# Depthwise convolution of the first batch: three tiles on TensorE in sixteen 32x32 array tiles, in place of one with 128x128 diagonals

## The chip, the cores and the metric

The kernel runs on one core of one Trainium2 chip. The metric is device time in microseconds (us), the lower the better. The measurement of this kernel can tell a change of about one per cent.

## What is computed

Two blocks in a row on x of shape (4, 256, 32, 32), all in float32:

```
# block 1, linear attention over heads of 8 channels
qkv = concat(wq, wk, wv) x                    # 768 channels
dw  = depthwise 5x5 convolution of qkv, SAME  # 25 taps per channel, weights per channel
pw  = 1x1 convolution of dw in groups of 8
f   = concat(qkv, pw) by heads: relu(query), relu(key), value with a column of ones
out = (value key^T) query, divided by its last row + 1e-15
y   = batch norm(proj out) + x
# block 2, attention over the 1024 pixels
out = o(h(y) softmax(f(norm y)^T g(norm y))) + y
```

## The kernel before

The four batch entries ("batches" 0 to 3) go through the core one after the other. The 768 channels of qkv are six tiles of 128 partitions: 0 and 1 hold the queries, 2 and 3 the keys, 4 and 5 the values. The images stand in `raw` with a border of zeros, so that a tap of the convolution is a shifted view (`tap_view`), and the sums go to `conv`.

Each engine has its order written out by hand; they meet at semaphores. `body(b)` is the stretch of one batch: pointwise convolution of keys and values (`pwkv`, L663), qkv of the next batch (`raw_kv`, L471 to L475), scores (L548), pointwise queries (`pwq`, L678 and L682), projection (L708), statistics and folding, then the attention of block 2: eight times energy (L605), softmax, transposes (L620) and values (L629). Ahead of `body(0)` stands a first stage for batch 0 alone: weights, qkv, and its convolution.

The convolution of batch b+1 runs beside `body(b)`, spread over three engines. VectorE multiplies and adds a tap in one instruction (`conv_taps`, L1143), for tiles 2, 3, 0 and the last eight taps of tile 1. For tiles 4 and 5 and seven taps of the shared tile 1, ScalarE makes a product (`conv_products`, L895) in one of five buffers, and GpSimd adds it (`conv_adds`, L1354); ScalarE waits for the addition that empties the buffer. Ten further taps of tile 1 ("late") go through ScalarE and GpSimd into a tile of their own inside `body(b)` (`late_products`, `late_adds`), and `pwq` adds that tile with a matrix product of its own (L682). Numbers in tables such as `FIRST_TAPS` say how many taps or products go between two other steps. The last `CARRY[b]` places of VectorE's list for batch b are done inside `body(b)`; the first 50 of the list are tiles 2 and 3.

Batch 0 has no body to hide its convolution, and divides it otherwise: tile 5 goes to TensorE. VectorE makes 25 diagonal matrices from the weights (L1314), and `diagonal_conv(h, first, last)` (L538) multiplies one half of the image, h, by one diagonal for each tap, all into one bank of PSUM; ScalarE copies it to `conv` (L924). The order on TensorE is

```
raw_q; diagonal_conv(0); scores; diagonal_conv(1, 0, 6); denominators; score_transposes;
diagonal_conv(1, 6, 12); fused_weights; spread 0; diagonal_conv(1, 12, 18); spread 1;
diagonal_conv(1, 18, 25); body(0)
```

Tile 1 of batch 0 has twelve taps on GpSimd in place of seven, and `body(0)` begins when VectorE has done tiles 2 and 3 and GpSimd all its 35 additions.

PSUM banks 0 to 3 are a ring (`a_slot`): each use has a running number, a bank is given out again when `a_free` has counted the use four numbers earlier, and `a_free` counts in order. `A_FIRST` is the number at the end of the first stage.

Of the kernel before, what the change touches and what calls it, by code (L numbers as in the profile page):

```python
# [6 lines left out]
ALU = mybir.AluOpType  # L7
# [5 lines left out]
P = 128  # L13
B = 4
C = 256
SIDE = 32
# [37 lines left out]
SHARED_TAPS, FIRST_SHARED_TAPS = 7, 12  # L54
# [8 lines left out]
PE_TILE = 5  # L63
PE_TAPS = [(PE_TILE, i) for i in range(NTAPS)]

SHARED_AT = 32

CARRY = (17, 16, 15, 2)
# [14 lines left out]
FIRST_POOL_SEQ = pool_order([tap for tap in ALL_TAPS if tap not in PE_TAPS], FIRST_SHARED_TAPS)  # L83
DVE_SEQ = [(t, i) for t in DVE_TILES for i in range(NTAPS) if (t, i) not in POOL_SEQ + LATE_SEQ]
DVE_TAPS, PRODUCTS = len(DVE_SEQ), len(POOL_SEQ)
KV_TAPS = sum(t not in Q_TILES for t, _ in DVE_SEQ)
# [4 lines left out]
POOL_ADDS = len(ADD_SEQ)  # L91
# [38 lines left out]
FIRST_TAPS = (42, 51, 57, 62)  # L130
FIRST_SPLIT = 29
# [5 lines left out]
FIRST_PRODUCTS_CONV = (16, 0)  # L137
FIRST_PRODUCTS_M = (3, 9, 15)
# [5 lines left out]
A_CONV = 2  # L144
CONV_BREAKS = (6, 12, 18)
# [12 lines left out]
def conv_seq_kernel(nc, x, wqkv, dw, pw, proj, bn, fgw, hw, ow, l1b, masks, out):  # L158
    with ExitStack() as ctx:
# [31 lines left out]
        mask_sb = sb("mask_sb", [P, 2 * P + HPT + CK * P])  # L191
# [18 lines left out]
        head_rows = mask_sb[:, 2 * P + HPT:].rearrange("p (h m) -> p h m", h=CK)  # L210
# [84 lines left out]
        def lay_out_mixed(b, at):  # L295
# [6 lines left out]
        a_end = lay_out(A_AT, [("raw_kv", A_RAWKV), ("kvt", A_KVT), ("raw_q", A_RAWQ), ("conv_0", A_CONV),  # L302
                               ("st_raw", 1), ("mb_raw", 1), ("conv_1", A_CONV)], 0, 0)
# [28 lines left out]
        def dve_count(b, n):  # L332
            return DVE_TAPS * b + n


        def product_count(b, n):
            return len(FIRST_POOL_SEQ) + (PRODUCTS + LATE) * b - PRODUCTS + n

        def add_count(b, n):
            return len(FIRST_ADD_SEQ) + (POOL_ADDS + LATE - 1) * b - POOL_ADDS + n  # L340

        def add_index(b, m):
            return add_count(b, m) if b else m
# [4 lines left out]
        def late_product_count(b, n):  # L348
            return product_count(b, PRODUCTS) + n

        def late_add_count(b, n):
            return add_count(b, POOL_ADDS) + n

# [26 lines left out]
        def conv_slot(h):  # L380

            return A_AT[f"conv_{h}", 0] + (A_CONV - 1 if h == 0 else 0)
# [20 lines left out]

        def diagonal(t, i):

            n = PE_TAPS.index((t, i))
            if n < 2 * NB:
                return ht[:, n // 2, n % 2 * P:(n % 2 + 1) * P]
            n -= 2 * NB
            return x1[:, n // NB, n % NB * P:(n % NB + 1) * P]  # L410
# [45 lines left out]
        def _(pe):  # L456
# [66 lines left out]
            def diagonal_conv(h, first, last):  # L523

                bank = a_bank(conv_slot(h))
                for i in range(first, last):
                    dst, view = square(bank), tap_view(PE_TILE, i)
                    y0, y1 = h * SIDE // 2, (h + 1) * SIDE // 2
                    if i > 0:

                        dy, dx = shift(i)
                        y0, y1 = max(y0, -dy), min(y1, SIDE - dy)
                        x0, x_end = max(0, -dx), SIDE - max(0, dx)
                        dst = dst[:, y0 - h * SIDE // 2:y1 - h * SIDE // 2, x0:x_end]
                        view = view[:, y0:y1, x0:x_end]
                    else:
                        view = view[:, y0:y1, :]
                    mm = pe.matmul(dst, diagonal(PE_TILE, i), view, start=(i == 0), stop=(i == NTAPS - 1))  # L538
                if last == NTAPS:
                    mm.then_inc(a_full, A_CONV)  # L540
# [113 lines left out]
            def body(b):  # L654
                with_next = b + 1 < B
                pe.wait_ge(conv_dve, dve_count(b, KV_TAPS))
# [14 lines left out]
                for i in range(A_PWQ):  # L671
# [7 lines left out]
                    if t == SHARED_TILE:  # L679
                        if h == 0:  # L680
                            pe.wait_ge(conv_pool, late_add_count(b, LATE - 1))
# [767 lines left out]
```

## Time and profile before

| | |
|---|---|
| time, median of 3 runs (lowest, highest) | 700.99 us (698.55, 703.51) |
| span of the profiled execution | 700.8 us |
| TensorE busy | 636.0 us (91%) |
| VectorE busy | 563.5 us (80%) |
| ScalarE busy | 470.7 us (67%) |
| GpSimd busy | 541.0 us (77%) |
| mean granted TensorE clock | 0.978 |

The profiled execution's own time is its span, 700.8 us; it lies 0.2 us under the median of the runs, so sums made on the span can be read as times. Busy shares are means over a first stage (to about 107 us), three bodies with the next batch's convolution beside them, and a last body without one, in which VectorE and ScalarE fall to two or three tenths and GpSimd stops. A float32 matrix product stands in the trace as two records, one for each pass; "PE" is the multiplication, "PEld" the load of its stationary operand.

### The profile page before, as it was taken

To read this page: it belongs to the slowest core of one execution; us is meant where nothing else is said; L and a number is where in the kernel's file an instruction comes from. 1 tells how busy PE (TensorE), PEld (TensorE's weight loads), DVE (VectorE), ACT (ScalarE), POOL (GpSimd) and SP (SyncE) were. 2 spreads that over 40 slices of the span, in tenths; PEclk is the share of its full clock that TensorE was granted. 3 is DMA by queue.
4 is the path that set the end of the run, shared out by engine and by line. 5 is a ranking of instruction groups with operands and counts; after the bars stand their busy time and mean duration, and the time that the engine had idled before them with its cause. 6 is when DMAs were issued, how large, how long until landed. Compare 5 with 4: busy or idle time off the path is not lost.

```text
span 700.8 us, 8645 instructions
## 1 busy us (share of the span) xinstructions
PE 636.0 (91%) x3176; PEld 475.3 (68%) x3176; DVE 563.5 (80%) x661; ACT 470.7 (67%) x745; POOL 541.0 (77%) x253
## 2 busy tenths in 40 slices
PE   4979978999989999999989999999898977997998
PEld 3854537665868787656778877648677773485887
DVE  5899899788989999989999998989999993442321
ACT  4787608897777769888676977987886662232231
POOL 4899996999999899999999999999999891000000
PEclk9979999999999999999999999999999998899999
DMA  8000001001010000001100000000100000000000
GB/s 296 2 0 1 0 0 61 1 1 34 27 61 15 16 31 1 0 1 60 61 1 16 16 31 1 1 0 1 61 15 16 9 22 1 0 1 0 16 16 30
DMA packets 6537, 16.23 MB, mean 23 GB/s; under 512 B 864, under 2 KB 992, under 8 KB 5984
## 3 DMA queue, kind: packets, MB, share of 16 engines
q1 hardware_dynamic: 6496, 15.69, 6.3%
q8 instruction: 25, 0.41, 0.2%
q14 instruction: 16, 0.13, 0.1%
HBM read 11.50 MB, written 4.19 MB: 22 GB/s over the span
## 4 chain that ended last, share of the span: by engine, by line
PE 36%; issue 20%; DVE 16%; ACT 15%; POOL 12%; DMA 1%; POOLq 0%; SPq 0%; DVEq 0%; ACTq 0%
DVE ps L1143 9%; PE ps L629 7%; PE ps L605 7%; ACT prod L895 7%; POOL conv L1354 7%; POOL rows L1354 4%; PE ps L538 4%; PE ps L708 3%; DVE small L1280 2%; PE ps L471 2%; PE ps L620 2%; ACT raw L864 1%; PE ps L756 1%; PE ps L475 1%; PE ps L472 1%
## 5 line engine op out<-in xcount | busy, mean ns | idle before, releaser
L1354 POOL TENSOR_TENSOR conv<-conv,prod 128x930 f32<-128x930 f32 (+4 forms) x197 | 432.4, 2238 | 16.0 <-ACT prod L895 13.2
L1143 DVE SCALAR_TENSOR_TENSOR ps<-raw,dw_sb,ps 128x930 f32<-128x930 f32 (+4 forms) x295 | 354.1, 1201 | 7.6
L895 ACT ACTIVATE prod<-raw,dw_sb 128x930 f32<-128x930 f32 (+4 forms) x233 | 250.2, 1123 | 16.6 <-POOL conv L1354 16.6
L629 PE MATMUL ps<-ht,pt 128*128 128x256 f32 x512 | 115.4, 379 | 2.7 <-ACT pt L1050 2.7
L629 PEld LDWEIGHTS ps<-ht,pt 128*128 128x128 f32 x512 | 95.0, 190 | 14.8 <-ACT pt L1050 3.1
L1041 ACT ACTIVATE rows<-ps,small 128x1024 f32<-128x1024 f32 x32 | 35.6, 1113 | 82.2 <-DVE small L1284 82.2
L1354 POOL TENSOR_TENSOR rows<-rows,prod 128x930 f32<-128x930 f32 (+4 forms) x27 | 62.9, 2329 | 9.9 <-ACT prod L895 6.5
L1280 DVE TENSOR_REDUCE small<-ps 128x1 f32<-128x1024 f32 x32 | 39.1, 1220 | 27.9 <-PE ps L605 27.8
L605 PE MATMUL ps<-hi,t_hi 128*128 128x512 f32 x128 | 45.3, 436 | 14.4 <-ACT rows L1041 14.4
L471 PE MATMUL ps<-hi,wqkv_hi 128*128 128x512 f32 x92 | 38.9, 423 | 4.4 <-ACT vt L910 4.4
L605 PE MATMUL ps<-lo,t_hi 128*128 128x512 f32 x128 | 41.2, 404 | 0.0
L605 PEld LDWEIGHTS ps<-hi,t_hi 128*128 128x128 f32 x128 | 23.7, 195 | 23.7 <-ACT rows L1041 18.6
L909 ACT ACTIVATE kt<-ps 128x256 f32<-128x256 f32 x68 | 31.6, 467 | 10.3 <-PE ps L665 10.3
L472 PE MATMUL ps<-hi,wqkv_lo 128*128 128x512 f32 x92 | 37.0, 402 | 0.0
L548 PE MATMUL ps<-vt,kt 128*128 128x129 f32 x272 | 32.1, 276 | 4.3 <-ACT vt L910 3.3
L620 PE MATMUL ps<-mask_sb,rows 128*128 128x128 f32 x256 | 33.4, 273 | 2.7 <-ACT pt L1050 2.7
L548 PEld LDWEIGHTS ps<-vt,kt 128*128 128x128 f32 x272 | 31.3, 192 | 6.5 <-ACT vt L910 5.7
L620 PEld LDWEIGHTS ps<-mask_sb,rows 128*128 128x128 f32 x256 | 29.2, 140 | 8.7 <-issue 3.8
L1297 DVE SCALAR_TENSOR_TENSOR x_t<-ps,small,x_t 128x256 f32<-128x256 f32 x32 | 15.1, 475 | 24.7 <-PE ps L629 24.7
L605 PE MATMUL ps<-hi,t_lo 128*128 128x512 f32 x128 | 34.8, 394 | 0.0
L1050 ACT COPY pt<-ps 128x512 f32<-128x512 f32 x64 | 33.9, 585 | 1.1 <-PE ps L620 1.1
L708 PE MATMUL ps<-q_raw,mb 128*128 128x512 f32 x64 | 32.5, 632 | 2.2 <-DVE lo L1238 1.5
(146 smaller groups left out, 1059.3 us busy)
## 6 DMA issues: line engine op xcount, KB each, us to landing
q_raw<-x_dram SPq DMA_DIRECT2D x8, 512.0 KB, 6.2
x<-x_dram SPq DMA_DIRECT2D x4, 1024.0 KB, 4.7
out_dram<-x_t SPq DMA_DIRECT2D x16, 256.0 KB, 2.3
conv<-wqkv_dram SPq DMA_DIRECT2D x1, 768.0 KB, 4.5
conv<-fg_dram SPq DMA_DIRECT2D x1, 512.0 KB, 5.1
proj_sb<-proj_dram SPq DMA_DIRECT2D x1, 512.0 KB, 7.6
pw_sb<-pw_dram SPq DMA_DIRECT2D x1, 384.0 KB, 6.1
mask_sb<-masks_dram SPq DMA_DIRECT2D x1, 264.0 KB, 6.2
```

Of the source, the lines that this page charges most:

```text
L471: pe.matmul(dst, lh, rh, start=(k == 0), stop=False)
L472: pe.matmul(dst, ll, rh, start=False, stop=False)
L548: mm = pe.matmul(dst[:, h * C:h * C + SCW], kt[:, j, h * P:(h + 1) * P], vt[:, j, h, 0:SCW], start=(j == 0), stop=(j == blocks - 1))
L605: mm = pe.matmul(ps[:, E_PAIR + h, :], lhs, m[:, h * HALF:(h + 1) * HALF], start=(s == 0), stop=(s == len(steps) - 1))
L620: mm = pe.transpose(ps[:, T_PAIR + u, j * P:(j + 1) * P], rows[:, i % ROW_BUFS, key:key + P], ident)
L629: mm = pe.matmul(dst[:, 0:C], pt[:, i % PT_BUFS, j, :], ht[:, j, :], start=(j == 0), stop=(j == NB - 1))
L708: mm = pe.matmul(dst, mb[:, k, c * P:(c + 1) * P], q[:, k % CK, h * HALF:(h + 1) * HALF], start=(k == 0), stop=(k == 2 * CK - 1))
L895: act.activation(dst, view, ACT.Copy, scale=weight(t, i)).then_inc(prod_ready, 1)
L1041: act.activation(rows[:, i % ROW_BUFS, :], ps[:, E_PAIR:E_PAIR + 2, :].rearrange("p a n -> p (a n)"), ACT.Exp, bias=neg_max[:, i:i + 1], a ...
L1143: return dve.scalar_tensor_tensor(dst, view, w, before, ALU.mult, ALU.add)
L1280: dve.tensor_reduce(neg_max[:, i:i + 1], ps[:, E_PAIR:E_PAIR + 2, :].rearrange("p a n -> p (a n)"), AX.X, ALU.max, negate=True).then_inc(r ...
L1354: pool.tensor_tensor(total, total, product, ALU.add).then_inc(conv_pool, 1)
```

## The change

For batch 0 three tiles, 5, 0 and 1, go to TensorE; VectorE keeps tiles 2 and 3 (50 taps), GpSimd tile 4 (25 products, 24 additions). There is no shared tile, no late tap and nothing carried into `body(0)`. The other batches are unchanged.

The array is used as sixteen tiles of 32x32. Row group r (channels 32r to 32r+31) and column group c: the stationary operand is a 32x32 diagonal of one tap's weights (`quad_weights`, made by three VectorE instructions), the moving operand is the view of that tap for 512 pixels, 32 partitions high. Column group c takes tap 4w+c in wave w, so six waves of sixteen products hold 24 taps; a seventh wave spreads the 25th tap over the four column groups, 128 pixels each. Row group r sums into bank r, so that a half tile fills all four banks of the ring, in each of them four partial sums of the same 32 channels. ScalarE copies the four banks to SBUF (`quad_sums`, in `x1` or `x1_t`, which are free), TensorE adds the four partial sums with a stacked identity of 128x32 (`whole_sums`), and ScalarE copies the whole to `conv`. A half tile is this step once; there are six. `body(0)` begins when all of them are copied.

```diff
-SHARED_TAPS, FIRST_SHARED_TAPS = 7, 12
+SHARED_TAPS = 7
-PE_TILE = 5
+PE_TILES = (5, 0, 1)
+FIRST_DVE_TILES = (2, 3)
+FIRST_POOL_TILE = 4
+QUAD = 32
-CARRY = (17, 16, 15, 2)
+CARRY = (0, 16, 15, 2)
-FIRST_TAPS = (42, 51, 57, 62)
-FIRST_SPLIT = 29
+FIRST_TAPS = (28, 33, 40, 45)
+FIRST_SPLIT = 14
-FIRST_PRODUCTS_CONV = (16, 0)
-FIRST_PRODUCTS_M = (3, 9, 15)
+FIRST_PRODUCTS_CONV = (2, 2, 2, 1, 0, 0)
...
-        a_end = lay_out(A_AT, [("raw_kv", A_RAWKV), ("kvt", A_KVT), ("raw_q", A_RAWQ), ("conv_0", A_CONV),
-                               ("st_raw", 1), ("mb_raw", 1), ("conv_1", A_CONV)], 0, 0)
+        a_end = lay_out(A_AT, [("raw_kv", A_RAWKV), ("kvt", A_KVT), ("raw_q", A_RAWQ),
+                               ("sums_5_0", QUADS), ("whole_5_0", 1), ("sums_5_1", QUADS), ("whole_5_1", 1),
+                               ("st_raw", 1), ("sums_0_0", QUADS), ("whole_0_0", 1), ("mb_raw", 1),
+                               ("sums_0_1", QUADS), ("whole_0_1", 1), ("sums_1_0", QUADS), ("whole_1_0", 1),
+                               ("sums_1_1", QUADS), ("whole_1_1", A_LAST)], 0, 0)
...
+            def quad_sums_of(t, h):
+                slot = A_AT[f"sums_{t}_{h}", 0]
+                banks = [a_slot(slot + r) for r in range(QUADS)]
+                for w in range(WAVES + 1):
+                    for c in range(QUADS):
+                        i = min(w * QUADS + c, NTAPS - 1)
+                        y0, rows_n, n0 = h * SIDE // 2, SIDE // 2, 0
+                        if w == WAVES:
+                            rows_n = SIDE // 2 // QUADS
+                            y0, n0 = y0 + c * rows_n, c * rows_n * SIDE
+                        for r in range(QUADS):
+                            k = slice(r * QUAD, (r + 1) * QUAD)
+                            mm = pe.matmul(banks[r][c * QUAD:(c + 1) * QUAD, n0:n0 + rows_n * SIDE],
+                                           quad_weights[t][k, TAP_ORDER[i], :], tap_view(t, i)[k, y0:y0 + rows_n, :],
+                                           start=(w == 0), stop=(w == WAVES))
+                mm.then_inc(a_full, QUADS)
+            def whole_sums(t, h):
+                n = whole_slots(t, h)
+                dst = a_slot(A_AT[f"whole_{t}_{h}", 0] + n - 1)
+                pe.wait_ge(a_free, A_AT[f"sums_{t}_{h}", 0] + QUADS)
+                for r in range(QUADS):
+                    mm = pe.matmul(dst[r * QUAD:(r + 1) * QUAD, :], quad_ident, quad_sums[h][:, r, :],
+                                   start=True, stop=True)
+                mm.then_inc(a_full, n)
...
+                if b == 0:
+                    pe.wait_ge(a_free, A_FIRST)
...
-            diagonal_conv(0, 0, NTAPS)
+            quad_sums_of(5, 0)
             scores(D_AT["sc_raw", 0], A_AT["kvt", 0] + A_KVT, RB)
-            diagonal_conv(1, 0, CONV_BREAKS[0])
+            whole_sums(5, 0)
+            quad_sums_of(5, 1)
             denominators(D_AT["den_raw", 0], D_AT["sc_raw", 0], q_raw[:, 0], A_AT["raw_q", 0] + A_RAWQ)
+            whole_sums(5, 1)
             score_transposes(A_AT["st_raw", 0], D_AT["sc_raw", 0])
-            diagonal_conv(1, CONV_BREAKS[0], CONV_BREAKS[1])
+            quad_sums_of(0, 0)
+            spread_denominators(D_AT["bc_raw", 0], 1, 0)
+            whole_sums(0, 0)
             fused_weights(A_AT["mb_raw", 0], A_AT["st_raw", 0], 0)
-            spread_denominators(D_AT["bc_raw", 0], 1, 0)
-            diagonal_conv(1, CONV_BREAKS[1], CONV_BREAKS[2])
+            quad_sums_of(0, 1)
             spread_denominators(D_AT["bc_raw", 0], 1, 1)
-            diagonal_conv(1, CONV_BREAKS[2], NTAPS)
+            whole_sums(0, 1)
+            quad_sums_of(1, 0)
+            whole_sums(1, 0)
+            quad_sums_of(1, 1)
+            whole_sums(1, 1)
...
+            def quad_sums_of(t, h):
+                slot = A_AT[f"sums_{t}_{h}", 0]
+                act.wait_ge(a_full, slot + QUADS)
+                for r in range(QUADS):
+                    act.copy(quad_sums[h][:, r, :], a_bank(slot + r)).then_inc(a_free, 1)
...
-            diagonal_conv(0)
+            quad_sums_of(5, 0)
             products(FIRST_PRODUCTS_CONV[1])
+            whole_sums(5, 0)
+            products(FIRST_PRODUCTS_CONV[2])
+            quad_sums_of(5, 1)
+            products(FIRST_PRODUCTS_CONV[3])
+            whole_sums(5, 1)
             score_transposes(A_AT["st_raw", 0])
...
+            quad_sums_of(0, 0)
+            whole_sums(0, 0)
             fused_weights(A_AT["mb_raw", 0], 0)
...
+            quad_sums_of(0, 1)
+            whole_sums(0, 1)
+            quad_sums_of(1, 0)
+            whole_sums(1, 0)
+            quad_sums_of(1, 1)
+            whole_sums(1, 1)
             products(PRODUCTS)
...
-            for t, i in PE_TAPS:
-                op = dve.tensor_scalar(diagonal(t, i), ident, weight(t, i), None, ALU.mult)
+            for t in PE_TILES:
+                op = dve.tensor_tensor(quad_weights[t], quad_ident.unsqueeze(1).to_broadcast([P, NTAPS, QUAD]),
+                                       dw_sb[:, t, :].unsqueeze(2).to_broadcast([P, NTAPS, QUAD]), ALU.mult)
```

`conv_taps`, `conv_products`, `conv_adds` and the counters behind them take the lists of batch 0 where they took the common ones; `late_products` and `late_adds` are empty for batch 0, and `pwq` of batch 0 has no second product.

## Rows read from the trace of the kernel before

**Rows 1.** Chain that ended last, first stage: start us, us, what.

```profile
52.22 20.30 PE ps L538 x50
...
100.29 7.13 PE ps L538 x14
```

**Rows 2.** TensorE in time: start, us, what, count [idle before, releaser].

```profile
52.22 12.79 PE L538 MATMUL ps<-raw,ht 128*128 128x512 f32 x32 [1.17 <-ACT raw L864]
...
72.36 4.18 PE L548 MATMUL ps<-vt,kt 128*128 128x129 f32 x36
...
87.74 1.02 PE L576 MATMUL ps<-proj_sb,s_t 128*128 128x256 f32 x4
...
107.25 0.60 PE L663 MATMUL ps<-pw_sb,conv 128*128 128x128 f32 x4
...
133.08 1.12 PE L682 MATMUL ps<-rows,pw_sb 128*128 128x512 f32 x2 [0.63 <-POOL rows L1354]
```

**Rows 3.** TensorE in time: attention of batch 0, and of the last batch.

```profile
194.50 0.62 PE L605 MATMUL ps<-hi,t_hi 128*128 128x512 f32 x2
...
259.65 0.61 PE L663 MATMUL ps<-pw_sb,conv 128*128 128x128 f32 x4
...
633.76 0.62 PE L605 MATMUL ps<-hi,t_hi 128*128 128x512 f32 x2
...
695.75 1.89 PE L629 MATMUL ps<-ht,pt 128*128 128x256 f32 x8
```

**Rows 4.** Windows, body 0: length, busy (instructions) of PE, PEld, DVE, ACT, POOL, clock.

```profile
107.00:260.00 153.00, 144.65 (x761) 111.19 (x761) 137.11 (x157) 122.68 (x191) 143.78 (x67) 0.99 0.07 27
```

**Rows 5.** Groups of TensorE lines in body 0: busy, mean ns, idle before, releaser.

```profile
L663 PE MATMUL ps<-pw_sb,conv 128*128 128x128 f32 x36 | 5.7, 280 | 1.2 <-ACT vt L910 1.2
...
L471 PE MATMUL ps<-hi,wqkv_hi 128*128 128x512 f32 x24 | 9.9, 412 | 0.6 <-ACT vt L910 0.6
```

**Rows 6.** Chain: eight float32 passes of 512 columns on the full array.

```profile
156.75 3.45 PE ps L708 x8
```

**Rows 7.** TensorE in time: sixteen passes on 128x32 column tiles, 256 columns each.

```profile
81.48 1.07 PE L567 MATMUL ps<-q_raw,kd 128*32 128x256 f32 x16
```

**Rows 8.** The same line, window 81.4 to 81.6 alone: count, duration ns, starts.

```profile
L567 PE MATMUL ps<-q_raw,kd x4: 403/403/403, 81.5 to 81.5; 128*32 128x256 f32 x4
```

**Rows 9.** TensorE in time: a long run of one-column products.

```profile
29.53 0.58 PE L813 MATMUL ps<-l1b_sb,conv 128*128 128x1 f32 x4
29.98 0.58 PE L810 MATMUL ps<-l1b_sb,conv 128*128 128x1 f32 x4
```

**Rows 10.** ScalarE in time: PSUM copies, splitting of the next input, products.

```profile
25.65 1.53 ACT L864 COPY raw<-ps 128x512 f32<-128x512 f32 x3
...
54.27 1.99 ACT L855 ACTIVATE hi<-q_raw 128x1024 fp32r<-128x1024 f32 x2
56.16 7.09 ACT L895 ACTIVATE prod<-raw,dw_sb 128x960 f32<-128x960 f32 x7
...
107.50 0.58 ACT L924 COPY conv<-ps 128x512 f32<-128x512 f32 x1 [12.69 <-PE ps L538]
```

**Rows 11.** GpSimd in time: additions of batch 0, late ones, batch 1.

```profile
18.52 35.40 POOL L1354 TENSOR_TENSOR conv<-conv,prod 128x900 f32<-128x900 f32 x15 [5.20 <-ACT prod L895]
...
86.39 4.66 POOL L365 TENSOR_TENSOR lo<-q_raw,hi 128x1024 fp32r<-128x1024 f32 x2
...
132.98 23.61 POOL L1354 TENSOR_TENSOR conv<-conv,prod 128x900 f32<-128x900 f32 x11
```

**Rows 12.** VectorE in time: first taps of batch 0.

```profile
20.40 1.29 DVE L1139 TENSOR_SCALAR ps<-raw,dw_sb 128x1024 f32<-128x1024 f32 x1 [3.19 <-ACT raw L864]
21.72 28.50 DVE L1143 SCALAR_TENSOR_TENSOR ps<-raw,dw_sb,ps 128x900 f32<-128x900 f32 x23
```

**Rows 13.** Windows, first stage: columns as in Rows 4.

```profile
97.00:101.00 4.00, 2.11 (x10) 1.11 (x11) 3.96 (x5) 0.00 (x0) 3.86 (x3) 0.98 0.00 0
101.00:104.00 3.00, 3.00 (x5) 1.35 (x4) 2.89 (x4) 0.00 (x0) 2.86 (x2) 0.50 0.00 0
```

More of the change, by code:

```diff
@@ L60 @@
 Q_TILES = (0, 1)
-PE_TILE = 5
-PE_TAPS = [(PE_TILE, i) for i in range(NTAPS)]
+PE_TILES = (5, 0, 1)
+FIRST_DVE_TILES = (2, 3)
+FIRST_POOL_TILE = 4
+QUAD = 32
+QUADS = P // QUAD
+WAVES = NTAPS // QUADS
 SHARED_AT = 32
-CARRY = (17, 16, 15, 2)
+CARRY = (0, 16, 15, 2)
 def pool_order(taps, shared=SHARED_TAPS):
@@ L82 @@
 POOL_SEQ = pool_order(ALL_TAPS)
-FIRST_POOL_SEQ = pool_order([tap for tap in ALL_TAPS if tap not in PE_TAPS], FIRST_SHARED_TAPS)
+FIRST_POOL_SEQ = [(FIRST_POOL_TILE, i) for i in range(NTAPS)]
 DVE_SEQ = [(t, i) for t in DVE_TILES for i in range(NTAPS) if (t, i) not in POOL_SEQ + LATE_SEQ]
-DVE_TAPS, PRODUCTS = len(DVE_SEQ), len(POOL_SEQ)
-KV_TAPS = sum(t not in Q_TILES for t, _ in DVE_SEQ)
+FIRST_DVE_SEQ = [(t, i) for t in FIRST_DVE_TILES for i in range(NTAPS)]
+PRODUCTS = len(POOL_SEQ)
 POOL_STARTS = [(t, 0) for t in POOL_TILES] + [(SHARED_TILE, LATE)]
@@ L90, with dve_seq, pool_seq, add_seq @@
 FIRST_ADD_SEQ = [tap for tap in FIRST_POOL_SEQ if tap not in POOL_STARTS]
-POOL_ADDS = len(ADD_SEQ)
+def dve_seq(b):
+    return DVE_SEQ if b else FIRST_DVE_SEQ
+def pool_seq(b):
+    return POOL_SEQ if b else FIRST_POOL_SEQ
+def add_seq(b):
+    return ADD_SEQ if b else FIRST_ADD_SEQ
+def late_seq(b):
+    return LATE_SEQ if b else []
+def late_adds_of(b):
+    return max(len(late_seq(b)) - 1, 0)
+def kv_taps(b):
+    return sum(t not in Q_TILES for t, _ in dve_seq(b))
 TAPS_SCORES_PW, TAPS_DEN_PW, TAPS_SCORES_RAW, TAPS_DEN_RAW = 8, 3, 1, 0
@@ L521, in kv_transposes @@
                 mm.then_inc(a_full, 1)
[L523 to L540, printed above, removed]
+            def quad_sums_of(t, h):
[14 more added lines that the diff above has]
+                mm.then_inc(a_full, QUADS)
@@ L897, in late_products @@
             def late_products(b, first, last):
-                for n in range(first, min(last, LATE)):
+                for n in range(first, min(last, len(late_seq(b)))):
                     if n > 0:
@@ L1361, in conv_adds @@
                     n = seq.index((t, i)) + 1
[L1362 removed]
+                    pool.wait_ge(prod_ready, product_count(b, n))
                     if (t, i - 1) in adds:
                         before = adds.index((t, i - 1)) + 1
[L1366 to L1367 removed]
+                        pool.wait_ge(conv_pool, add_count(b, before))
+                    add(conv[:, t, :], add_count(b, m), i)
             def late_adds(b):
[L1371 removed]
+                for m in range(late_adds_of(b)):
                     pool.wait_ge(prod_ready, late_product_count(b, m + 2))
@@ L1424 @@
     masks = np.concatenate([np.eye(P), np.kron(np.eye(HPT), np.ones((D, D))), np.kron(np.eye(HPT), np.ones((D, 1))),
-                            head_rows], 1).astype(np.float32)
+                            head_rows, np.tile(np.eye(QUAD), (QUADS, 1))], 1).astype(np.float32)
     arrays = {
```

123 lines of the change are left out of this document (55 added, 68 removed).

## The prediction

> **What bounds the kernel now.** I read the chain of work that ended last first, because a change to the first stage counts only by when `body(0)` can start. From 52.22 us the chain lies on TensorE: 20.30 us of diagonal products, and in the end 7.13 us more, up to 107.42 us [rows 1]. TensorE in time shows what follows: the first pointwise product of `body(0)` at 107.25 us [rows 2]. So the first stage ends with the last diagonal product, and VectorE's and GpSimd's shares of batch 0, large as they are, are not what ends it.
>
> Then I asked what bounds a body, for only then is an earlier or later start worth its full length. The attention of batch 0 takes from 194.50 to 259.65 us, 65.2 us, with the next convolution beside it on three engines. The last batch has nothing beside it, and takes from 633.76 to 697.64 us, 63.9 us [rows 3]. The engines beside it make almost no difference: TensorE's own order sets it. In `body(0)` TensorE is busy 144.65 of 153.00 us, GpSimd 143.78, VectorE 137.11 [rows 4]; the three are close. I take TensorE as the bound, and a shift of the start of `body(0)` as a shift of the end; GpSimd as the bound is a rival.
>
> **The change part by part.** Up to 52.22 us, where the last query image is drained, nothing on TensorE's path moves. The 25 small diagonal instructions on VectorE become three larger ones; they end before 20.40 us, where VectorE waits 3.19 us for its first image [rows 12], so I cost them at nothing; that wait would cover 3 us more of them.
>
> *Removed from the other engines.* VectorE loses 28 of 78 taps, about 1.2 us each [rows 12]; its 50 take some 62 us from 20.40 us, with a few small steps and waits between, so it is done near 102 us. GpSimd loses 11 additions in the first stage and 9 late ones: 14 additions by 51.6 us at 2.36 us each, the splitting of the next input after ScalarE's 56.3 us, then 10 more at 2.2 us, done near 82 us [rows 10, 11]. Neither gives time as long as TensorE's six steps end later. VectorE at 102 us is late next.
>
> *Added: six steps, each in this order.*
> 1. Sums: a float32 pass of 512 columns takes 3.45 / 8 = 0.431 us [rows 6]. Nothing shows sixteen 32x32 tiles at once; the nearest row is four column tiles: sixteen passes of 256 columns in 1.07 us [rows 7], where one after another they would take 16 x 0.216 = 3.4 us, and four of them start within the same tenth of a microsecond [rows 8]. So I take a wave as two passes of 0.431 us with all sixteen tiles together: six waves 5.17 us, the seventh (128 columns) 0.22, the end of the last pass 0.2: 5.6 us. Below that it can't fall, since the passes of one tile follow each other. From above: 32 pairs of load and product stand in each wave, 224 in a step, and the only long run of pairs starts four in 0.45 us, 0.11 us a pair [rows 9], 24.9 us a step; there each load has 128 columns, here 32, so I take the near row and keep the far one for the range.
> 2. ScalarE copies four banks: three in 1.53 us [rows 10], 2.0 us for four.
> 3. Whole: two passes with four column tiles at once, 0.86 + 0.2 = 1.1 us.
> 4. ScalarE copies the whole: 0.6 us [rows 10].
> Four hand-overs at 0.08 us (diagonal's end at 107.42, copy at 107.50 us [rows 1, 10]) make 0.3. A step is 9.6 us. Steps don't overlap: the sums ask for all four banks of the ring, and the last of these comes free only when the whole before has been copied. Six steps are 57.6 us.
>
> *Beside the steps.* `scores` (4.18 us [rows 2]) stands after the first sums and hides only 2.0 us of copies: +2.2. Between the first sums' copies and the first whole's copy ScalarE has two products. The second of them, number 22, waits for addition 16 (five buffers); GpSimd splits until 60.0 us and has addition 16 at 64.4 us, so the whole is copied at 66.1, not 63.9 us: +2.2. `fused_weights` (1.02 us [rows 2]) with its copy holds up the ring once, `score_transposes`, shorter, is taken alike: +2.0. Spread and denominators lie in copies. `body(0)` starts at 52.2 + 57.6 + 6.4 = 116.2 us, against 107.25 us: +8.9 us. If all three hid, it would be 109.8 us, +2.5.
>
> *The clock.* In the stretch 97 to 101 us TensorE was busy for 2.11 of 4 us, and in the next 3 us its granted clock was 0.50, the lower level of 1.2 GHz [rows 13]. In a step TensorE works 6.7 of 9.6 us with a gap of 2 us. I take two such stretches in six steps, 1.5 us lost in each: +3.0 us, with none and one in each step (9 us) as bounds.
>
> *Taken out of `body(0)`.* The late products leave ScalarE: TensorE waited 1.2 and 0.6 us for its copies there [rows 5]. The second product of `pwq`, four passes of 0.43 us, goes, with a wait of 0.63 us for GpSimd [rows 2]: 1.8 + 1.7 + 0.6 = 4.1 us. At least nothing; at most all 8.35 us of TensorE's idle time [rows 4] and the 1.7.
>
> Sum against the profiled execution: 700.8 + 8.9 + 3.0 - 4.1 = 708.6, taken as 709 us; that execution lies 0.2 us from the median of the runs.
>
> The Trainium skill (TensorE: Matmul & The Clock Gate, Part 1, "Wait — 56ns, not 53.3ns?") says that starts of small matmuls never come closer than about 25 ns. By it the 32 passes of the seventh wave would take 0.8 us, not 0.22, an estimate from that page: 3.5 us more in six steps, 712 us. The four starts in a tenth of a microsecond [rows 8] don't decide it, being rounded; I leave it in the range.
>
> **The rivals.**
> *Feeding (0.2).* TensorE's order can't be fetched and started as fast as sixteen tiles use it up. For it: no row holds a faster long run than 0.11 us a pair [rows 9]; at that rate the sums take 24.9 us and the six steps 116 us more, 825 us; at half of it 12.4 us, 41 us more, 750 us. Against it: the burst of rows 7, though that is only 32 instructions.
> *The tiles take turns (0.02).* The change doesn't do what it says: the second pass of a product must start before another tile's first, so that a wave is 16 x 0.431 = 6.9 us, a step about 47 us and the whole 930 us. Against it: eight products on four column tiles would then take 9 x 0.216 = 1.9 us, and took 1.07 us [rows 7].
> The Trainium skill (the same page, Part 3, "The mechanism") has the multiplications in strict program order, start and end; with both passes of a product next to each other this rival would follow. The measured 1.07 us speaks against it.
> *GpSimd is the bound (0.15).* Its run of additions for batch 1 starts at 132.98 us [rows 11], behind nine late ones. Without those it starts when the first value tiles of batch 1 are drained, some 16.5 us after the start of `body(0)` (eight pointwise blocks of 0.67 us, six units of qkv at 1.38 us, a copy and two products): 116.2 + 16.5 = 132.7 us, as before; with the clock's 3.0 us 135.7. If that run sets the end, 700.5 to 703.5 us, no change. Against it: the attention of rows 3.
> *Faster: ScalarE held `body(0)` (0.13).* If all TensorE's idle time there comes from ScalarE's late products and what they push back, 8.35 + 1.7 = 10.1 us go in place of 4.1; with no clock loss 700.8 + 8.9 - 10.1 = 699.6, and 697 us if the wait for addition 16 goes too. It decides from the point where the body loses more than the stage gains. Against it: only 1.8 of 8.35 us is put down to ScalarE at these lines [rows 5].
>
> **How the numbers follow.** The forecast has 0.5: 700 to 719 us by its bounds (clock 0 to 9 us, body 0 to 10 us). The predicted time is 709 us. From 697 us (ScalarE) to 735 us (the lower part of Feeding) leaves out 0.2: most of Feeding, turns, and a little below. One per cent, about what a measurement of this kernel can tell from no change, is 694 and 708 us. Faster: tails of the ScalarE rival and of the forecast's lower bounds, 0.1. Within: the GpSimd rival, the rest of ScalarE's, and the part of the forecast without clock loss, 0.4. Slower: the rest of the forecast, Feeding, turns, 0.5.
>
> **What would show it.** Right: sums of 5 to 6 us, six steps of 9 to 11 us, `body(0)` at 114 to 120 us, VectorE and GpSimd idle before it for some 14 and 34 us, body lengths unchanged but for the first. Sums near 12 or 25 us show Feeding; 40 us, turns. `body(0)` late and the end unmoved shows GpSimd. Wrong I would be if the sums were fed slowly, if the clock fell in every step, or if some step overlapped the next after all.

## The result, and the profile after

The changed kernel takes 719.66 us (median of 5 runs, 715.10 to 719.99), the kernel before 700.99 us: 1.0244 times as long, 95% interval 1.0206 to 1.0282. Forecast were 709 us and a range of 697 to 735. Ratios leave out an execution that is over 1.5% longer than the fastest of its kernel. The direction and the range held; the loss was forecast at 8 us and is 17 to 19. That the time lies in the range owes something to luck: the forecast's own bounds ended at 719 us, and the room above them was kept for Feeding, which is not what happened.

TensorE in time, changed kernel (start, us, line, operands, count, in brackets the idle time before and who ended it):

```profile
49.44 6.99 PE L558 MATMUL ps<-raw,ht 32*32 32x512 f32 x224 [1.26 <-ACT raw L904]
56.35 4.29 PE L579 MATMUL ps<-vt,kt 128*128 128x129 f32 x36
60.57 1.06 PE L569 MATMUL ps<-x,mask_sb 128*32 128x512 f32 x8
63.44 6.99 PE L558 MATMUL ps<-raw,ht 32*32 32x512 f32 x224 [1.80 <-ACT conv L972]
...
109.05 6.99 PE L558 MATMUL ps<-raw,pt 32*32 32x512 f32 x224 [0.79 <-ACT conv L972]
118.27 1.07 PE L569 MATMUL ps<-x_t,mask_sb 128*32 128x512 f32 x8 [2.23 <-ACT x_t L966]
120.29 1.19 PE L696 MATMUL ps<-pw_sb,conv 128*128 128x128 f32 x4 [0.95 <-ACT conv L972]
...
270.64 0.61 PE L696 MATMUL ps<-pw_sb,conv 128*128 128x128 f32 x4
```

The reader is to see one step in the lines from 109.05 to 120.29: sums (L558), a gap in which ScalarE copies four banks, whole (L569), a gap for the copy of the whole, and the first pointwise product of `body(0)` (L696). All six sums take 6.99 us in this execution; they were forecast at 5.6. `body(0)` starts at 120.29 us, in place of 107.25 [rows 2]; batch 1's body at 270.64, in place of 259.65 [rows 3].

ScalarE in time, the same kernel, steps one and six:

```profile
61.73 1.10 ACT L935 ACTIVATE prod<-raw,dw_sb 128x960 f32<-128x960 f32 x1 [1.38 <-POOL conv L1407]
62.73 0.57 ACT L972 COPY conv<-ps 128x512 f32<-128x512 f32 x1
...
116.07 2.05 ACT L966 COPY x_t<-ps 128x512 f32<-128x512 f32 x4 [7.17 <-PE ps L558]
119.44 0.59 ACT L972 COPY conv<-ps 128x512 f32<-128x512 f32 x1 [1.32 <-PE ps L569]
```

These are the forecast's 2.0 and 0.6 us of copies, and in step one the product that waits for GpSimd ahead of the copy of the whole. VectorE and GpSimd in time, the first work of each in `body(0)`:

```profile
141.96 0.42 DVE L1232 TENSOR_TENSOR s_masked<-ps,mask_sb 128x256 f32<-128x256 f32 x1 [39.24 <-PE ps L579]
```

```profile
138.38 6.36 POOL L1407 TENSOR_TENSOR conv<-conv,prod 128x900 f32<-128x900 f32 x3 [57.89 <-ACT prod L935]
```

VectorE was done at 102.7 us and GpSimd at 80.5: 17.6 and 39.8 us before `body(0)` starts.

The forecast's sum against this trace, in spans:

| term | forecast | measured | difference |
|---|---|---|---|
| last drained image, where the sums begin | 52.22 | 49.44 | -2.8 |
| six sums | 6 x 5.6 = 33.6 | 6 x 6.99 = 41.9 | +8.3 |
| the rest of six steps | 6 x 4.0 = 24.0 | 6 x 4.09 = 24.5 | +0.5 |
| scores, product's wait, fused weights and others | 6.4 | 4.4 | -2.0 |
| start of `body(0)` | 116.2 | 120.3 | +4.1 |
| clock in the steps | +3.0 | 0 in this execution | -3.0 |
| `body(0)` shorter | -4.1 | 150.35 - 152.40 = -2.05 | +2.05 |
| later bodies | 0 | 442.46 - 441.15 = +1.3 | +1.3 |
| span | 708.6 | 713.1 | +4.5 |

Two things don't show in this table. Every run lists a time 1.7 to 2.0 us above its span; the forecast took the span for the time, which is 2 us. And the two traced executions aren't typical ones: the span of the changed kernel has a median of 716.2 us over nine executions (713.1 is the least of them), that of the kernel before 697.3 us over the 36 that ran beside the experiments (695.1 to 704.1; the traced one has 700.8). So the traces show 12.3 us of a difference that is 17 in the times. The first row of the table is of this kind, and not of the change: in the run without late taps below, whose first stage is that of the kernel before, the diagonal products start at 49.59 us and `body(0)` 55.0 us later, the same 55.0 as from 52.22 to 107.25 us [rows 2]. Between 40 and 52 us the granted clock was 1.00 in that run and 0.72 in the trace of the kernel before. Chain against chain, the changed kernel's 70.85 us are 15.8 us more, where 8.9 and 3.0 for the clock were forecast.

### The profile page after: what moved, and what is told of

Same layout as the page of the kernel before. It is cut to its first block, busy times and chain, and to the rows that moved or that the text cites. A ratio compares the mean times of both kernels' runs of the same rounds, so it can differ in the third digit from the quotient of the medians.

```text
span 713.1 us, 11152 instructions
## 1 busy us (share of the span) xinstructions
PE 642.6 (90%) x4464; PEld 485.0 (68%) x4464; DVE 527.5 (74%) x611; ACT 464.2 (65%) x751; POOL 496.9 (70%) x233
## 4 chain that ended last, share of the span: by engine, by line
PE 39%; issue 20%; DVE 15%; ACT 13%; POOL 12%; DMA 1%; SPq 0%; POOLq 0%; DVEq 0%; ACTq 0%
DVE ps L1202 8%; PE ps L660 7%; POOL conv L1407 7%; PE ps L636 7%; PE ps L558 5%; ACT prod L935 5%; POOL rows L1407 4%; PE ps L742 3%; DVE small L1332 2%; PE ps L493 2%; PE ps L494 2%; PE ps L651 2%; PE ps L497 2%; PE ps L790 1%; PE ps L579 1%
## 5 line engine op out<-in xcount | busy, mean ns | idle before, releaser
L1407 POOL TENSOR_TENSOR conv<-conv,prod 128x930 f32<-128x930 f32 (+4 forms) x186 | 408.7, 2233 | 78.7 <-ACT prod L935 75.6
L1202 DVE SCALAR_TENSOR_TENSOR ps<-raw,dw_sb,ps 128x930 f32<-128x930 f32 (+4 forms) x271 | 325.3, 1200 | 6.7
L935 ACT ACTIVATE prod<-raw,dw_sb 128x930 f32<-128x930 f32 (+4 forms) x213 | 228.8, 1124 | 4.9 <-POOL conv L1407 4.9
L1407 POOL TENSOR_TENSOR rows<-rows,prod 128x930 f32<-128x930 f32 (+4 forms) x18 | 41.8, 2322 | 2.3
L1232 DVE TENSOR_TENSOR s_masked<-ps,mask_sb 128x256 f32<-128x256 f32 x8 | 3.4, 420 | 47.5 <-PE ps L579 47.5
```

Source lines behind the costliest of these rows:

```text
L935: act.activation(dst, view, ACT.Copy, scale=weight(t, i)).then_inc(prod_ready, 1)
L1202: return dve.scalar_tensor_tensor(dst, view, w, before, ALU.mult, ALU.add)
L1407: pool.tensor_tensor(total, total, product, ALU.add).then_inc(conv_pool, 1)
```

## The experiments

**Other executions of the changed kernel.** No edit.

> The changed kernel once more, unaltered. The profiled execution (715.10 us, span 713.1, mean granted clock 0.976) is the shortest of its five; the others have spans of 716.8 to 718.0 at clocks of 0.967 to 0.971. If the difference is TensorE's clock, every execution follows one line: a clock lower by 0.007 is 0.007 x 717 = 5 us more of full-clock work missing, so 4 to 5 us more span, and the trace of a longer execution shows the same six steps of 11 to 14 us (body 0 at 120 to 122 us) with some 9 us more at the granted clock of 0.50. Rival: the longer executions have longer steps or waits at the same clock; then body 0 starts later than 122 us, or the clocks don't order the spans. Time 715 to 720 us under both.

Median 716.86 us (4 runs), ratio 1.0243 (1.0204 to 1.0283); the traced execution has a span of 715.1 us at a mean clock of 0.971. TensorE in time, its last step, and the windows view of 108 to 125 us (length, busy and count of PE, PEld, DVE, ACT, POOL, granted clock, DMA):

```profile
108.18 8.49 PE L558 MATMUL ps<-raw,pt 32*32 32x512 f32 x224 [0.79 <-ACT conv L972]
118.91 1.94 PE L569 MATMUL ps<-x_t,mask_sb 128*32 128x512 f32 x8 [2.23 <-ACT x_t L966]
121.80 1.19 PE L696 MATMUL ps<-pw_sb,conv 128*128 128x128 f32 x4 [0.95 <-ACT conv L972]
```

```profile
108.00:125.00 17.00, 13.63 (x247) 8.65 (x248) 0.00 (x0) 3.60 (x9) 0.00 (x0) 0.71 0.15 45
```

Here the clock did fall in a step: the sums take 8.49 in place of 6.99 us, the whole 1.94 in place of 1.07, 2.4 us together, at waits that are the same to 0.05 us. The chain from the first sums to `body(0)` is 73.2 us, against 70.85. Over all executions the clock orders the spans roughly, within each kernel: of the kernel before, three at 0.968 have spans of 702.9 to 704.1 us and three at 0.983 of 695.4 to 696.4, 7 us for 0.015 (executions at 0.985, with 697.6 to 699.1, don't fit). The median clock is 0.980 before and 0.971 after; at 7 us for 0.015 that is 4 us. So the expectation holds in kind: by this estimate the clock costs the changed kernel 2 to 4 us in most executions. In the first one traced it costs the steps nothing; there it fell just after them, to 0.53 between 120.0 and 123.5 us.

**Half the columns.** In waves one to six:

```diff
-                        if w == WAVES:
+                        if w < WAVES:
+                            rows_n = SIDE // 4
+                        else:
                             rows_n = SIDE // 2 // QUADS
```

> The first six waves of each sum stream 256 columns in place of 512, so half of each image's sums is left out; the number of instructions stays. Theory (feeding): the 448 loads and products of a step come at about 15 ns each once what was fetched ahead is used up, so the sums keep 6.6 to 7.0 us. As the prediction had it (streaming): 12 passes of 0.216 us, 0.22 and 0.2, 3.0 us. Rival (a fixed loss between the passes of one tile, (6.99 - 5.6) / 12 = 0.12 us): 12 x 0.33 + 0.4 = 4.4 us. Start of body 0: 120 us under feeding, 120 - 6 x 4 = 96 (then 103, when VectorE is done) under streaming, 6 x 2.6 = 16 us earlier, 104 us, under the rival.

Sums of 5.2 to 5.7 us at full clock: none of the three. TensorE in time, fourth sums, and the windows view of the third sums, their line alone (length, busy and count of PE, of PEld, clock, DMA):

```profile
83.34 3.96 PE L560 MATMUL ps<-raw,ht 32*32 32x256 f32 x187 [0.77 <-ACT mb L960]
87.48 1.05 PE L560 MATMUL ps<-raw,ht 32*32 32x256 f32 x37 [0.18 <-issue]
```

```profile
72.52:72.95 0.43, 0.42 (x32) 0.33 (x33) 1.00 0.00 0
72.95:73.60 0.65, 0.65 (x58) 0.52 (x34) 1.00 0.00 0
```

The windows are cut at the first start of each wave, and some 32 loads (the second count) are one wave of sixteen tiles. The first wave takes 0.43 us, its two passes of 0.216; the following ones 0.65. The same cut through the changed kernel's second sums:

```profile
63.43:64.29 0.86, 0.85 (x32) 0.35 (x33) 1.00 0.00 0
64.29:65.36 1.07, 1.07 (x49) 0.61 (x34) 1.00 0.00 0
...
69.65:70.43 0.78, 0.77 (x36) 0.42 (x22) 1.00 0.00 0
```

0.86 us for the first wave, 1.07 for the others. So a wave after the first costs 0.21 us more than its two passes, whether these are long or short. That is no fixed time per instruction (the waves would stay at 1.07) and not the columns. But between the 177th and the 201st product of four of the six shortened sums TensorE stands idle, with no engine named that it waits for (issue), 0.18 to 1.05 us: at this pace, 3.96 us for 374 loads and products, the instructions do run short.

The starts of single records show where the 0.21 us lies. In the changed kernel's later waves the two passes of a product start 0.45 us apart (64.486 and 64.938 us), close to the 0.43 of a pass; the next product on the same tile, by the order, starts 0.62 us after (65.557). So streaming itself is hardly slowed; the next wave comes late.

**The last tap in one column.**

```diff
-                for w in range(WAVES + 1):
-                    for c in range(QUADS):
...
+                taps = [(0, NTAPS - 1)] + [(i % QUADS, i) for i in range(NTAPS - 1)]
+                for n, (c, i) in enumerate(taps):
+                    for r in range(QUADS):
...
+                        mm = pe.matmul(banks[r][c * QUAD:(c + 1) * QUAD, :], quad_weights[t][k, TAP_ORDER[i], :],
```

> The 25th tap is done first, as four products of 512 columns in the first column of tiles, in place of sixteen of 128 columns at the end: 400 instructions a step in place of 448. Feeding: 400 x 15 ns = 6.0 and the last pass 0.43, so sums of 6.3 to 6.5 us, 0.5 to 0.7 us less in each of six steps, body 0 some 3 to 4 us earlier and the time 3 to 4 us shorter (715.5 to 717 beside 719.7). A fixed loss between the passes of one tile: the tiles of the first column have 14 passes of 0.55 us, 7.7 us, and the steps grow by 0.7 us, the time by 4 us.

A miss for feeding: 400 instructions in place of 448, and the sums take 7.43 us; 720.16 us, ratio to the kernel before 1.0301 (1.0253 to 1.0349). The windows view of the third sums, their line alone:

```profile
75.02:75.88 0.86, 0.86 (x26) 0.49 (x30) 1.00 0.00 0
75.88:76.74 0.86, 0.86 (x29) 0.44 (x12) 1.00 0.00 0
76.74:77.82 1.08, 1.08 (x41) 0.62 (x35) 1.00 0.00 0
```

The four products of the extra tap and the sixteen of the first wave use 1.72 us, and 42 loads start in that time; without the extra tap 33 start in 0.86. The first column's tiles are used twice in a row, four passes of 0.43 us, so its four products of the first wave wait for the extra tap. Behind these stand twelve products on free tiles: eight of them start at once (75.08 to 75.13 us), the last four only from 75.63 to 76.12 us, by the counts and the order, since the trace names no tile. So TensorE passes by a product that waits, but only so far: the four of the extra tap, the four that wait and the eight that pass them are sixteen products, 64 loads and multiplications. The total lies near the fixed loss's 14 passes of 0.55 us, 7.7 us, but the windows show that the loss isn't between all passes: it is in the first two windows and then 0.21 us a wave.

**Without tile 1.** The last two steps are taken out of TensorE's and ScalarE's order:

```diff
             whole_sums(0, 1)
-            quad_sums_of(1, 0)
-            whole_sums(1, 0)
-            quad_sums_of(1, 1)
-            whole_sums(1, 1)
```

> The last two of the six steps are left out, so that tile 1 of the first batch isn't computed (its pointwise product takes tile 0 in its place). Theory (the chain of steps on TensorE sets the end): the chain ends at 98 us, but the pointwise products also wait for VectorE's 50 taps, done at 102.7 us; body 0 starts at 102.5 to 104 us in place of 120.3, and all of these 16 to 18 us are gone from the end: 699 to 703 us. Rival (GpSimd or VectorE bounds the bodies): less than 10 us are gone from the end, 707 us or more.

696.26 us (10 runs), ratio 0.9958 (0.9924 to 0.9991), a little below the expectation. TensorE in time:

```profile
95.98 1.07 PE L568 MATMUL ps<-x_t,mask_sb 128*32 128x512 f32 x8 [0.83 <-ACT x_t L961]
...
102.63 1.22 PE L695 MATMUL ps<-pw_sb,conv 128*128 128x128 f32 x4 [5.58 <-DVE conv L1193]
```

Now VectorE's taps, not the steps, let `body(0)` start, at 102.63 us: 17.7 us earlier than in the changed kernel, and the span is 19.5 us shorter. The start sets the end, to within 2 us, and GpSimd isn't the bound. All traces say so (start of `body(0)`, span, us):

```
kernel                     start    span    span - start
before                    107.25   700.8   593.5
changed                   120.29   713.1   592.8
changed, again            121.80   715.1   593.3
half the columns          113.74   706.8   593.1
last tap in one column    125.21   716.7   591.5
without tile 1            102.63   693.6   591.0
eight tiles               128.52   722.4   593.9
twelve tiles              122.43   715.2   592.8
split columns             144.65   739.3   594.6
before, no late taps      104.61   694.6   590.0
tiles 5 and 3, second      98.18   689.8   591.6
```

**Eight tiles.**

```diff
-                        for r in range(QUADS):
+                        for r in range(QUADS // 2):
```

> Two of the four row groups are left out, so half of each tile's channels isn't summed: eight tiles work in place of sixteen, and each has its 12 long passes as before. A wave of sixteen tiles was seen to take 1.07 us where the two passes of a tile last 0.86. Theory (starts): the passes of a wave start at best 16.7 ns apart and in order, so that the tiles fall behind each other; with 16 passes in a wave the loss halves, 0.96 us a wave, sums of 6.1 to 6.4 us. Rival (each tile loses 0.1 us between its passes, whatever the others do): 12 x 0.53 us and the last tap, 6.6 to 6.9 us. Pure streaming, as predicted, would be 5.4 to 5.6.

5.61 us: the time predicted for streaming, and below what both theories of the loss gave. The windows view of the third sums, their line alone (some 16 loads are a wave now):

```profile
76.61:77.47 0.86, 0.86 (x24) 0.36 (x16) 1.00 0.07 19
...
80.92:81.40 0.48, 0.45 (x24) 0.17 (x8) 1.00 0.00 0
```

Every wave takes its two passes, and the last tap 0.45 us. No loss belongs to a tile by itself; it needs more than eight. Nor were the theory's 16.7 ns a floor: the passes of a first wave start 7 ns apart. Yet the time is 724.32 us (one run): from 95 us on, with sums at the same place in the order, the granted clock was 0.50 (windows, columns as in [rows 4]):

```profile
95.00:133.00 38.00, 30.91 (x270) 11.51 (x263) 5.84 (x5) 7.42 (x16) 0.00 (x0) 0.51 0.08 29
```

**Twelve tiles.** The same edit with `range(QUADS - 1)`.

> One of four row groups is left out, so a quarter of each tile's channels isn't summed: twelve tiles, 24 passes in a wave. Seen so far: sums of 5.61 us with eight tiles (the predicted time) and 6.99 us with sixteen. Theory (the starts of a wave's passes, one after the other, add up to a loss that grows with their number): between the two, 6.1 to 6.5 us at full clock. Rival (the loss belongs to the sixteen, because four row groups write into four banks on the same partitions at once): 5.6 us, or in proportion to the row groups, 6.3 us, which the theory gives as well; then the next run decides.

6.00 us at full clock, a little below the theory's 6.1 and above the 5.6 of the rival. TensorE in time, and one wave in the windows view:

```profile
74.92 6.00 PE L558 MATMUL ps<-raw,ht 32*32 32x512 f32 x168 [0.69 <-ACT s_t L954]
```

```profile
76.64:77.50 0.86, 0.86 (x40) 0.58 (x25) 1.00 0.00 0
```

24 passes go into 0.86 us without loss; the 0.4 us over eight tiles lie in the last tap, 0.84 in place of 0.45 us. So the loss doesn't grow evenly: it appears between 24 and 32 passes in a wave. Four row groups and 32 passes come together here, so this run alone doesn't part them. Against the row groups speaks the first wave of the sixteen, which writes all four banks at once and takes 0.86 us. In this run too the clock fell, to 0.74 from 95 to 123 us, so that `body(0)` starts at 122.43 us in spite of the shorter sums.

**Split columns.** In waves two to six each product is issued as two halves:

```diff
-                for w in range(WAVES + 1):
+                for w, p in [(0, 0)] + [(w, p) for w in range(1, WAVES) for p in range(2)] + [(WAVES, 0)]:
...
+                        if 0 < w < WAVES:
+                            rows_n = SIDE // 4
+                            y0, n0 = y0 + p * rows_n, p * rows_n * SIDE
```

> All taps done; in waves two to six each product of 512 columns is issued as two of 256, so that the columns streamed stay and the instructions nearly double. A wave of sixteen tiles was seen to cost 0.21 us more than its two passes both at 512 columns (1.07 beside 0.86) and at 256 (0.65 beside 0.43). Theory (a loss for each wave of 32 starts): 6.99 + 5 x (2 x 0.65 - 1.07) = 8.1 us a step, and more if instructions run short as with half the columns. Body 0 starts 7 us or more later, 127 to 130 us, and the end is as much later. Rival (a loss for each column streamed by sixteen tiles at once): sums of 7.0 us, body 0 and the end as in the changed kernel.

741.19 us; `body(0)` starts at 144.65 us, far above either. TensorE in time, third sums:

```profile
77.59 3.04 PE L561 MATMUL ps<-raw,ht 32*32 32x512 f32 x113 [0.69 <-ACT s_t L957]
80.94 2.75 PE L561 MATMUL ps<-raw,ht 32*32 32x256 f32 x128 [0.31 <-issue]
84.39 2.61 PE L561 MATMUL ps<-raw,ht 32*32 32x256 f32 x128 [0.71 <-issue]
87.84 0.45 PE L561 MATMUL ps<-raw,ht 32*32 32x128 f32 x15 [0.84 <-issue]
```

The same columns as in the changed kernel, and 10.7 us in place of 7.0. Between two stops the waves of 256 columns go as with half the columns: 0.43 us for the first, 0.62 to 0.68 for the next (starts at 80.94, 81.37, 82.04, 82.66 us). Two such waves are some 1.3 us where one of 512 columns took 1.07, so the loss is not one per column. The rest are the stops. After each 128 products, with their loads 256 instructions, TensorE stands idle for 0.3 to 0.8 us, with no engine named that it waits for (0.2 to 1.3 us over all six sums). 256 instructions each 3.45 us are 13.5 ns for one. The pages of the two kernels, this one and the changed one, have a row for a DMA queue of instructions (packets, MB, share):

```profile
q8 instruction: 43, 0.70, 0.4%
q8 instruction: 35, 0.57, 0.4%
```

Eight packets more, of 16 KB each, stand against 1920 loads and products more (5424 and 5424 by the page, against 4464 and 4464), 240 for one packet, and in the third sums a packet starts between each two stops (78.60, 82.08 and 85.42 us). So the stops are likely waits for instructions to be fetched; that is argued, not shown. The changed kernel's sums use 448 in 6.99 us, 15.6 ns, and have no such gap. So Feeding exists, but just beyond the changed kernel's pace. The 8.1 us expected from the wave's loss alone can't be read from the total.

**What the change takes out of `body(0)`, alone.** In the kernel before, without the late taps of batch 0:

```diff
-                for n in range(first, min(last, LATE)):
+                for n in range(first, min(last, LATE * (b > 0))):
...
-                for m in range(LATE - 1):
+                for m in range((LATE - 1) * (b > 0)):
```

with the counts of products and additions and the second product of `pwq` to match.

> The kernel before without the ten late products, nine late additions and the second product of the last query tile in batch 0, so that ten taps of one tile of that batch are left out: what the change takes out of body 0, alone. As predicted: body 0 starts at 107.25 us as before and is 4.1 us shorter, 697 us beside 701. Rival (the changed kernel's body 0 was only 2.3 us shorter in its trace, clock stretch included): 1 to 2.5 us shorter, 699 us. Rival (GpSimd holds the body): its additions for batch 1 start 10 us or more earlier, and body 0 is shorter by over 6 us.

698.50 us (10 runs), ratio 0.9966 (0.9929 to 1.0003). TensorE in time:

```profile
104.61 0.60 PE L663 MATMUL ps<-pw_sb,conv 128*128 128x128 f32 x4
...
253.32 0.61 PE L663 MATMUL ps<-pw_sb,conv 128*128 128x128 f32 x4
```

`body(0)` lasts 148.7 us here, against 152.4 [rows 2, 3]: 3.7 us, the predicted term in place. The whole run gains 0.34%, 2.4 us, and by the interval anything from nothing to 5 us. In this trace batch 1's body, up to 404.72 us, is 151.4 us long, against 150.05, so 1.4 us come back there, and from the start of `body(0)` to the end it is 3.5 us shorter.

**Tiles 5 and 3.** The lessons put together. The start of `body(0)` needs tiles 2 to 5; tiles 0 and 1 are needed only by `pwq`. So TensorE gets 5 and 3, VectorE 2, 0 and part of 1, GpSimd 4 and the late taps of 1:

```diff
-PE_TILES = (5, 0, 1)
-FIRST_DVE_TILES = (2, 3)
+PE_TILES = (5, 3)
+FIRST_DVE_TILES = (2, 0, 1)
...
-FIRST_DVE_SEQ = [(t, i) for t in FIRST_DVE_TILES for i in range(NTAPS)]
+FIRST_DVE_SEQ = [(t, i) for t in FIRST_DVE_TILES for i in range(NTAPS) if (t, i) not in LATE_SEQ]
...
-    return LATE_SEQ if b else []
+    return LATE_SEQ
...
+            late_products(0, FIRST_LATES[0], sum(FIRST_LATES[:2]))
```

> All taps done, shared out anew in the first batch: TensorE sums tiles 5 and 3 (four steps), VectorE tiles 2 and 0 and fifteen taps of tile 1, GpSimd tile 4 and then ten late taps of tile 1, whose products ScalarE makes between the steps. Body 0 needs of VectorE only tile 2 at its start. Theory (the steps set the start of body 0, and the start the end): the four steps end at 98 us and body 0 starts there, 22 us before the changed kernel's 120.3, and with tile 1 done by 110 us nothing is late in the body: 719 - 22 = 695 to 698 us, some 4 us below the kernel before. Rival (a body that starts so early waits for the other engines): tile 1's taps or GpSimd's additions end later than the query products ask for them, and 5 us or more come back: 700 to 706 us.

Median 690.70 us (688.35, 689.11, 692.30 and, traced, 699.62), ratio to the kernel before 0.9829 (0.9762 to 0.9895): below the 695 to 698 us expected, which took the start from the changed kernel's trace (715.10 us in time) and the time from its median. The traced execution is the longest of the four, so the rows shown are those of the next run, in which two products also move:

```diff
-FIRST_PRODUCTS_CONV = (2, 2, 2, 1, 0, 0)
+FIRST_PRODUCTS_CONV = (2, 0, 4, 1, 0, 0)
```

> All taps done, shared out as in the run with tiles 5 and 3, and two of ScalarE's products that stood between the first sums and the copy of the first whole are made after it. Theory: the wait of TensorE ahead of the second sums, 1.8 us, goes, body 0 starts 1.8 us earlier, and the time is 1 to 2 us below that kernel's 690.7 us, 687 to 690 us; the ratio to the kernel before is 0.98. Rival (GpSimd, given its products later, holds up the late additions that the query product waits for): no gain or a loss of up to 3 us, 690 to 694 us.

690.92 us (6 runs, 688.98 to 691.66), ratio 0.9869 (0.9836 to 0.9901). TensorE, VectorE and GpSimd in time:

```profile
61.60 6.99 PE L558 MATMUL ps<-raw,ht 32*32 32x512 f32 x224 [0.80 <-ACT conv L967]
...
98.18 0.68 PE L696 MATMUL ps<-pw_sb,conv 128*128 128x128 f32 x4 [0.90 <-DVE ps L1196]
```

```profile
104.07 1.28 DVE L1196 SCALAR_TENSOR_TENSOR conv<-raw,dw_sb,ps 128x1024 f32<-128x1024 f32 x1
118.41 0.42 DVE L1226 TENSOR_TENSOR s_masked<-ps,mask_sb 128x256 f32<-128x256 f32 x1 [13.07 <-PE ps L579]
```

```profile
93.81 14.07 POOL L1401 TENSOR_TENSOR rows<-rows,prod 128x930 f32<-128x930 f32 x6 [0.48 <-POOL rows L1401]
```

`body(0)` starts at 98.18 us, 9.1 us before the kernel before, and the other engines are done at 105.4 and 107.9 us, ahead of the query products. TensorE's wait before the second sums fell from 1.80 to 0.80 us as expected, but the third sums of this execution lost 1.5 us to the clock, and the two versions' times can't be told apart: the second half of the expectation isn't borne out. Either is faster than both kernels, by the intervals, which end below 1.

## Why the prediction was wrong in size

- **What bounds the kernel: right.** The time from the start of `body(0)` to the end is 590 to 595 us in eleven traces with starts from 98.2 to 144.7 us. The GpSimd rival, in which the start doesn't reach the end, is out, and so is the ScalarE rival: `body(0)` was to lose 10.1 us, and lost 2.05, or 3.7 alone.
- **The sums: the step that failed.** "So I take a wave as two passes of 0.431 us with all sixteen tiles together": 5.6 us predicted, 6.99 measured, 8.3 us in six steps and the largest error. The row it rested on, sixteen passes on four tiles [rows 7], was a burst of 32 instructions, as the rival said; the first wave of the sums, 0.86 us, is exactly as predicted, and so are all waves with eight tiles (5.61 us in all) and twelve. From the second wave on, sixteen tiles lose 0.21 us in each, 1.05 us a step; the last tap, with short passes, takes 0.77 in place of 0.42 us, 0.35 more. Why sixteen lose and twelve don't wasn't isolated. That the pace of instructions alone isn't it, half the columns shows; that streaming is hardly slowed, the starts of its passes show; that TensorE passes by a waiting product only within some sixteen products, the last tap in one column shows. The likeliest reading is that TensorE looks ahead over a limited stretch of its order, and that 32 passes with their loads fill it; no run varied this by itself, so it is argued, not shown.
- The Trainium skill (TensorE: Matmul & The Clock Gate, Part 3, "The mechanism") gives TensorE a reorder window of 64 instructions. A wave of sixteen tiles is 64, of twelve 48, of eight 32: the loss of 0.21, 0 and 0 us agrees, and so do the sixteen products, 64 instructions, that the last tap in one column reached over. Its rule that multiplications keep strict program order, by which a wave would take 6.9 us, is contradicted by 0.86 and 1.07 us. The floor of 25 ns between starts (the same page, Part 1, "Wait — 56ns, not 53.3ns?") fails as well: 32 passes with their loads go into a first wave of 0.43 us with half the columns, 13 ns a pass.
- **Feeding, as a rival: not the cause here, but near.** No idle time put down to issue stands in the changed kernel's sums at 15.6 ns an instruction; with more or shorter products it does. Its price of 0.11 us a pair was too high by a factor of 3.5 even for the sums as they are (6.99 us for 224 pairs, 0.031 us); the products it was taken from [rows 9] load 128 columns each, these 32.
- **The rest of a step: right.** Copies 2.05, whole 1.06, copy 0.59, hand-overs 0.39: 4.09 us against 4.0. Steps don't overlap, as argued from the ring.
- **Beside the steps: 2 us too much.** `scores` and the product's wait were added up, 4.4 us; the longer sums push the scores to where GpSimd is nearly ready, and together they cost 2.9. `score_transposes` and `fused_weights` cost 1.3 us, not 2.0.
- **The clock: about right in size, its place by chance.** No fall in the steps of the first traced execution, 2.4 us in the second, some 4 us by the medians of the clocks; 3.0 was forecast. It also taxes a repair: with quicker sums the clock stood at 0.51 for 38 us (eight tiles) and at 0.74 for 28 us (twelve), in one execution each.
- **`body(0)`: right alone, half of it lost in the changed kernel.** Without the late work it is 3.7 us shorter (4.1 predicted); in the changed kernel 2.05, where its first products run at the lower clock (1.19 us for four passes, in place of 0.60 [rows 2]), and the later bodies give back 1.3 us: 0.7 us of 4.1 reach the end in this trace.
- **The signs.** VectorE and GpSimd idle ahead of `body(0)` for 17.6 and 39.8 us (14 and 34 named), and its start, at 120.3 us, at the edge of 114 to 120; the sums above 5 to 6 us and steps of 11.1 to 14.0 above 9 to 11 showed that the sums were off.
- **Span and time.** Taking the span as the time left out 2 us, and the two traces, one at the long end and one at the short end of their kernels' executions, hide 5 us of the difference.

In the traced execution (715.10 us, forecast 708.6) some 6.5 us were missed: 8.3 for the sums, 0.5 for the rest of the steps, 3.4 for the bodies and 2.0 for the span, less 2.0 beside the steps, 2.8 for the earlier start and 3.0 for the clock. The rest of the 9 to 11 us by which the loss was missed are differences between executions: the earlier start, which isn't the change's, and, by the estimate above, most of the clock.

## What to carry to other kernels

A row that shows a burst prices a burst: before a rate is carried to a run ten times as long, look for the longest run of that kind in the trace, and if there is none, let the price grow after the first burst and keep that in the forecast, not only in the range. When work is moved to another engine, ask when each piece is needed, and keep off the chain what the start of the next stage doesn't need: here the same taps, shared out by when they are needed and with two tiles on TensorE in place of three, gained 1.3% where the change lost 2.4%. Compare medians of several executions, with their clocks, before a difference of a few microseconds between two traces is explained.

## What the runs showed of the hardware

- Sixteen 32x32 float32 tiles run together, 32 passes of 512 columns in 0.86 us at first, then in 1.07 us; twelve tiles keep 24 passes in 0.86 us throughout.
- TensorE starts products on free tiles past others that wait for a busy tile, but not without limit: with four products waiting, eight behind them started at once, and four more, also on free tiles, 0.5 to 1.0 us later.
- TensorE's instructions ran short when they were used faster than about 13.5 ns each: idle stretches of 0.2 to 1.3 us after some 256 (split columns); at 15.6 ns each there were none.
- With half the tiles at work and the same order, the granted clock was 0.51 over 38 us, against 0.99 in the changed kernel's first stage from 49 to 121 us and 0.71 over 17 us of it in another execution. How much of this is the tiles was not isolated.
